# A four-convolution graph network: one block of nodes moved from the dense matrix to the gathered part

## The reference

```
edge_index = stack([src, dst])
h = max(layernorm(x), 0); x = x + L0(h)   # two GATv2 layers: softmax over each target's edges, then sums
h = max(layernorm(x), 0); x = x + L1(h)   # one GCN layer, then a layer norm
h = max(layernorm(x), 0); x = x + L2(h)   # gelu((h[src] + edge_attr) @ W1.T) * bases, summed per target; two norms
h = max(layernorm(x), 0); x = x + L3(h)   # three GCN layers with a skip

def _gcn_conv(x, W, b, src, dst, ew, n):  # used three times in L3; L1 is of the same form
    deg  = segment_sum(ew, dst);  dinv = rsqrt(deg)
    norm = dinv[src] * ew * dinv[dst]
    return segment_sum((x @ W)[src] * norm[:, None], dst) + b
```

## Time and profile before

| | us |
|---|---|
| median of 3 runs | 6614.33 (6613.65 to 6617.98) |
| profiled execution | 6613.22 |
| its span | 6611.4 |
| mean granted clock of PE | 0.760 |

### The profile page before, as it was taken

How to read it: one execution, slowest core, us unless ns; L and a number is a source line. 1 busy time by engine, 2 the same in 40 slices (tenths; PEclk the granted TensorE clock), 3 DMA queues, 4 the chain that set the end, 5 groups by cost and what they waited for, 6 DMA issues and landing times. The chain is left out here.

```text
span 6611.4 us, 98533 instructions
## 1 busy us (share of the span) xinstructions
PE 4901.7 (74%) x22849; PEld 3470.2 (52%) x22849; DVE 4012.6 (61%) x12754; ACT 2179.0 (33%) x5456; POOL 4554.9 (69%) x4402
## 2 busy tenths in 40 slices
PE   3677775457766766555996995666666799999998
PEld 2344443246654444433766995555555455555555
DVE  7998996589976676334776446444444644444444
ACT  4344444359943343343773003222222400000000
POOL 1777777688877777777877662777777177376474
PEclk9555556579965555556997997777777799999999
DMA  5988865457744444333555883655555299899897
GB/s 203 296 297 288 280 183 149 124 105 143 143 71 108 107 106 95 80 81 63 87 84 159 288 286 114 174 160 160 160 160 151 77 303 305 287 305 301 290 305 254
DMA packets 922048, 1211.81 MB, mean 183 GB/s; under 512 B 256572, under 2 KB 658496, under 8 KB 908602
## 3 DMA queue, kind: packets, MB, share of 16 engines
q1 hardware_dynamic: 601694, 867.12, 41.0%
q0 software_dynamic: 205952, 221.31, 17.1%
q10 hardware_dynamic: 113836, 117.04, 5.2%
HBM read 970.24 MB, written 235.93 MB: 182 GB/s over the span
## 5 line engine op out<-in xcount | busy, mean ns | idle before, releaser
L1182 POOL DMA_INDIRECT ACC<-table,TABS x1760 | 1664.8, 946 | 610.1 <-issue 610.1
L1497 POOL DMA_INDIRECT BUF<-table,TABS x888 | 841.7, 948 | 560.8 <-issue 257.0
L1263 POOL DMA_INDIRECT adjacency<-TABS x584 | 934.8, 1601 | 242.2 <-issue 214.4
L1803 POOL DMA_INDIRECT TABS<-table,SPOT_SRC x836 | 788.8, 944 | 317.9 <-issue 317.6
L1988 PE MATMUL picked<-BUF,G 128*128 x2368 | 582.1, 426 | 440.9 <-DVE ACC L2014 386.5
L1988 PEld LDWEIGHTS picked<-BUF,G 128*128 128x128 f32 x2368 | 513.7, 320 | 675.0 <-issue 675.0
L2491 PE MATMUL asum<-BUF 128*128 128x144 f32 x3520 | 558.4, 303 | 122.4 <-DVE BUF L2463 100.2
L1826 PE MATMUL pre<-wmat,BUF 128*128 128x128 f32 x1672 | 325.9, 356 | 357.0 <-DVE BUF L1852 346.8
L1996 DVE TENSOR_TENSOR picked<-picked,ACC 128x512 f32<-128x512 f32 (+1 forms) x440 | 247.3, 562 | 545.2 <-DMA ACC<-table,TABS 499.2
L2491 PEld LDWEIGHTS asum<-BUF 128*128 128x128 f32 x3520 | 472.9, 196 | 197.7 <-issue 180.1
L1212 DVE TENSOR_TENSOR ACC<-ACC,asum 128x144 f32 (+1 forms) x1760 | 463.0, 263 | 151.5 <-DVE ACC L1212 65.0
(11 more groups left out here) (466 smaller groups left out, 9968.3 us busy)
## 6 DMA issues: line engine op xcount, KB each, us to landing
TABS<-adjacency SPq DMA_DIRECT2D x264, 512.0 KB
BUF<-in_edge_pair SPq DMA_DIRECT2D x836, 128.0 KB
BUF<-adjacency SPq DMA_DIRECT2D x99, 1024.0 KB
BUF<-adjacency SPq DMA_DIRECT2D x198, 512.0 KB
adjacency<-zeros ACTq DMA_DIRECT2D x44, 1792.0 KB
G<-adjacency SPq DMA_DIRECT2D x132, 512.0 KB
kept<-ACC SPq DMA_DIRECT2D x220, 272.0 KB, 4.4
G<-kept SPq DMA_DIRECT2D x220, 272.0 KB
```

The source lines that it names most:

```text
L1182: po.indirect_dma_start(rows[:, slot, j, 0:width], None, tab, bass.IndirectOffsetOnAxis(ap=SRC[:, q * GT + j:q * GT + j + 1], axis=0)).the ...
L1263: po.indirect_dma_start(adj_flat, bass.IndirectOffsetOnAxis(ap=PLACE[:, k:k + 1], axis=0), TOTAL[:, k:k + 1], None, compute_op=ALU.add).th ...
L1497: po.indirect_dma_start(R[:, q % deep_ring, j, :], None, table, bass.IndirectOffsetOnAxis(ap=SRC[:, k:k + 1], axis=0)).then_inc(S(f"gather ...
L1803: po.indirect_dma_start(R[:, g % RD, j, :], None, table, bass.IndirectOffsetOnAxis(ap=SPOT_SRC[:, k:k + 1], axis=0)).then_inc(S(f"gathered ...
```

## The change

LIGHT goes from 16 to 17, so 17 blocks are gathered and 32 are dense. From this follow: NEAR 74 to 78 groups, FAR 146 to 142, HEAVY 33 to 32, chunks (DENSE) 9 to 8; the chunk of one block is gone, and the part of one block is now the last light part (the fifth), while the last part is four blocks wide. The adding groups are spread anew by FIRST_FAR and MERGES: 1, 10, 60, 9 in the first GAT layer (before 1, 11, 60, 10), 1, 2, 50 in the second (before 1, 3, 49), and 9 in front of the mixed stage (before 11). In the mixed stage near groups come every 1.1 units (before 1.3), the last at unit 90 of 104 (before 100 of 108); in the last stage every 2.2 units (before 2.5), the last at unit 181 of 200 (before 194 of 207), which is in the last chunk, and the assertion that it lies ahead of the last chunk is replaced.

```diff
--- before.py
+++ after.py
@@ -57,13 +57,13 @@
 CD = 8
 
 CYCLE = NB - 1
-LIGHT = 16
+LIGHT = 17
 HEAVY = NB - LIGHT
 assert SORT_T + NB - 1 <= TILES
 NEAR_TILES = LIGHT * (SORT_T + CYCLE - 1) // CYCLE
 NEAR = -(-NEAR_TILES // (2 * GT)) * 2
 FAR = GROUPS - NEAR
-FIRST_FAR = 82
+FIRST_FAR = 80
 SEGMENTS = ((0, FIRST_FAR), (FIRST_FAR, FAR))
 DENSE = -(-HEAVY // CB)
 PARTS = ([(b, min(CB, LIGHT - b)) for b in range(0, LIGHT, CB)]
@@ -73,7 +73,7 @@
 FIRST = (6, 6, 0)
 BY_VECTOR = 24
 ONES_FROM = 160
-MERGES = ((1, 11, 60, 10), (1, 3, 49, 11))
+MERGES = ((1, 10, 60, 9), (1, 2, 50, 9))
 assert FAR % 2 == 0
 
 
@@ -1288,7 +1288,7 @@
                 w = min(CB, HEAVY - c * CB)
                 deep = CB * CB // w
                 units += [(c, w, b, min(deep, NB - b)) for b in range(0, NB, deep)]
-            places = near_by(6, 1.3)
+            places = near_by(6, 1.1)
             assert places[-1] < len(units)
             added, after_add, after_dense = [0], {}, {}
             finished, total = [], st[0][:, 0:NB]
@@ -1453,8 +1453,8 @@
                 units += [(c, w, b, min(deep, NB - b)) for b in range(0, NB, deep)]
             US = len(units)
             ends = {c: max(n for n, u in enumerate(units) if u[0] == c) for c in range(DENSE)}
-            places = near_by(12, 2.5)
-            assert places[-1] < ends[DENSE - 2]
+            places = near_by(12, 2.2)
+            assert places[-1] + 1.3 * KS < US
             loops_at = {6 + 2 * i: i for i in range(FREE_PARTS)}
             advance_at, n = {}, places[-1] + 3
             for k in range(KS - 1):
```

## The result

The changed kernel takes 6653.15 us (median of 5, 6644.88 to 6660.11) against 6614.33 before: 1.0061 times as long, 95% interval 1.005 to 1.0071. It is slower by about 39 us, where +11 was forecast; the range ended at 6639. The profiled execution, 6660.11 us, is the slowest of the five, 7 us above the median.

The account below looks back on a forecast made before the run. POOL's gathers were to replace PE as the last stage's bound. Last stage +25.7, mixed stage -4.1, stage ends -7.4 and -3.0 sum to +11.2 on the profiled 6613.2, stated as 6625 us; range 6600 to 6639.

Parts of the forecast that it names:

- the bound: Last stage's three passes: POOL's gathers, no longer PE, set each pass's last near product, together +22.7 us.
- The final +3.0: Behind the third pass: the last part is four blocks and not one, +3.0 us (+1.5 to +5).
- the tail at 0: Last near product to each pass's end: length unchanged, 0, between -1.2 a pass and +3.
- the chain of shifts: Last-stage tails: twelve parts of DVE steps, loads and ACT shifts, about 3.3 us a part, put at 43.6 us.
- rival C: Last-stage tails: the chain of shifts, at 3.6 us a part, adds +4 a pass, +12, giving 6637 us; 23%.
- the transition: Last stage, last advance to the next pass's first gather: no term in the forecast, 0.
- the 7.2 us saved: Last stage: PE's work falls 7.2 us a pass, which becomes waiting as it lies ahead of the last near product.
- 20-odd us of thin products: Last stage before the change: part of the 43.9 us from last near product to the pass's end.
- The stage ends: Stage ends with adding groups: fewer POOL steps, -7.4 us in the second dense stage, -3 behind the first maximum.
- The mixed stage: Mixed stage: POOL sets the last near product, chunk 6's add comes first, finish costs +3.0; -4.1 us in all.
- A: Whole kernel: PE stays the bound, with POOL's step under 4.65 us a group; 6563 us; 8%.
- B: Whole kernel: passes cost only +14, mixed stage and stage ends gain in full, -8 and -15; 6605 us; 17%.

Follow-up runs that it names:

- the kernel with fewer gathers: The changed kernel gathering three tiles and not four per group in the last stage, from the first pass's seventh group on (fourth tile stale): 6568.49 us.
- runs without rows: Last-stage dinv row loads left out except the first two (stale rows used): 6622.43 us on the changed kernel, 6592.92 on the kernel before.
- four rows: A ring of four dinv rows and not two, each row asked for two parts earlier: 6629.57 us on the changed kernel, 6592.72 on the kernel before.
- stores first: The changed kernel with the next pass's first two dinv rows loaded behind the last part's store, not ahead of the last three stores: 6642.86 us.
- the four-block store before the change: The kernel before, its last part's store in the first two passes writing four blocks and waiting for the stores ahead of it: 6611.63 us.
- the kernel with 2.4: The kernel before (16 blocks) with near groups every 2.4 units in the last stage and every 1.15 in the mixed stage: 6623.06 us.
- the best one: The kernel before with a ring of four dinv rows and only five parts finished ahead of the mixed stage's add: 6582.14 us.

## Why the prediction was wrong

**Right: the bound.** POOL sets the last near product, +23.5 against +22.7; its step stayed 1.25 us, PE waits 18 us a pass for gathers, and the kernel with fewer gathers is 85 us faster. The final +3.0 was +3.1.

**Wrong: the tail at 0, "between -1.2 a pass (PE alone) and +3".** It grew by 10.6 over the three passes. PE alone was worked out rightly: 42.7 and three units are the 47.9 of the runs without rows and with four. The term that failed is the chain of shifts, taken over from before less two steps: the twelfth shift was to end 41.5 - 1.4 = 40.1 after the near product, and it ended 44.4, 42.5 and 48.0 after it. Its pace is no property of the chain: it waits for rows that land beside the unit loads. With four rows the same shift ends 36.2, 36.3 and 39.4 after the near product. That was rival C, whose sign, place and mechanism were right; its 12 us were 10.6. That they came so close is in part luck: C had +4 in each pass, and the passes have +2.5, -0.8 and +8.9. The third pass loads no units of a next one, and there the unit loads beside the chain went from 5 to 11 and the rows' mean landing from 3.9 to 5.0 us; in the second, 16 loads and not 13 made the rows no later on average. I gave C 23% and let it stand alone.

The wait for rows explains why the forecast of the tail missed, but not why the change is slower, since the kernel before has this wait too (21 us of its tails, against 18 after). With four rows in both, the change still costs 37 us, 6629.57 against 6592.72: 25.7 to the last near product, 13.6 in the tails, 9.3 in the transitions.

**Wrong: no cost for the transition.** The forecast has no term for the way from the last advance to the next first gather. It became 13.5 us longer over two passes. Of 6.8 a pass, 4.4 go when the stores stand ahead of the next pass's rows, and 2.3 when the last store is of one block; both were asked in runs of their own, and that they add up was not tried. The rows were ahead of the stores before too, but earlier: before, the second row's load went out 6.3 us ahead of the last store (5718.07 and 5724.36) and had landed when that store was issued, at 5722.2; after, it went out 4.6 us ahead (5722.76 and 5727.35) and landed at 5729.8, behind the store's issue (landings by the semaphore's updates in the trace; the second pass's end shows the same order). From the last store's issue to POOL's first gather it takes 5.3 and 5.6 us before, 6.5 and 6.2 there with four blocks stored, 7.0 and 6.8 after the change with the stores first, 9.1 and 8.7 with one block behind the rows, and 11.3 and 11.1 with four blocks behind them. So 5.7 of the 6.8 are the landing of the last stores, and 1.1 the wider last advance with its move; 4.4 and 2.3 are more than 5.7, so the two causes overlap.

**The step that failed beneath both** is the sentence that the 7.2 us saved "lie ahead of the last near product", followed by a sum in which everything behind it stays as it is. The thin products are not ahead of it: they are units 200 to 206, and the last near group stood at unit 194. (The prediction's "20-odd us of thin products" are 11 us; the 20 are all products of the tail before.) By the prices of rows 3, as an estimate, what goes from ahead of it is 26 wide products less the new groups and the loop block, 18.5 us a pass, and PE waits 18.1 for gathers. Behind it PE's own work grows from 32.0 us (11 wide products, 49 thin ones, twelve advances, the near group) to 42.7. Before, PE spent most of that difference waiting for shifts; after, it works, and the wait for rows still comes on top.

With PE as the bound, POOL's lead covers a late first gather, as the four-block store before the change shows (transition longer, time the same). With POOL as the bound each pass is a closed ring: first gather, last gather, tail, stores, first gather. Every link counts in full.

**The rest, about right.** The stage ends were put at -10.4. The second logits' first gather came at 1937.3 on average over the seven profiles with 17 blocks (1933.0 to 1944.6) and at 1946.3 over the seven with 16 (1942.9 to 1952.8): -9.0, though the two profiles compared first show only -2.1. The mixed stage was put at -4.1 and is -1.1 from its first gather to L2's (530.7 against 531.9 on average; the kernel with 2.4 and the best one, where that stage differs, left out): the near products ended as forecast, but the last chunk took 45.6 us and not 43.8, and the wait before it 2.2. Together -9.0 - 1.1 + 50.7 = +40.6, and the medians differ by 38.8.

The faster rivals A and B fell with the 395 us of the gathers.

## What to carry to other kernels

When a change hands the bound from one engine to another, work out the new engine's whole loop, with the transfers that close it, and not only the stretch in which it takes over: what the old bound had hidden is paid from then on. A chain's pace read from a trace holds for the transfers that ran beside it; where the change puts more of them there, bound it anew. Count what stands behind the last step that the new bound sets: what is moved there is paid too. And before moving work between two engines, look at what small loads wait for: asking for four rows ahead and not two was worth 19 us in the kernel before, with no work moved.

## What the runs showed of the hardware

The sums stage of the first layer does the same work in all these kernels, and it is through sooner where the granted clock of PE is higher (the clock of a stretch is a mean: its records show 1.0 or 0.5, which is 2.4 or 1.2 GHz). The same stretch before, after, and in the run without rows (the last three columns are the clock, the DMA share and GB/s):

```profile
1395.00:1840.00 445.00, 347.88 (x2108) 298.74 (x2108) 407.84 (x1684) 405.98 (x1273) 373.55 (x230) 0.95 0.71 142
```

```profile
1395.00:1840.00 445.00, 354.43 (x2077) 304.75 (x2075) 402.11 (x1658) 399.06 (x1251) 372.88 (x231) 0.92 0.70 140
```

```profile
1395.00:1840.00 445.00, 345.79 (x2136) 296.09 (x2135) 412.74 (x1707) 410.50 (x1287) 374.48 (x228) 0.96 0.72 144
```

At 0.92 PE gets through 2077 instructions in the stretch, at 0.96 through 2136. The second logits' start moved over 11.6 us between the seven profiles with 17 blocks, which are alike up to there, more than the stage ends were worth: it was 1944.6 and 1943.6 at the two lowest clocks, 0.92 and 0.93, and 1933.0 to 1936.3 at 0.95 to 0.99. Such a gain can't be read from one pair of traces. At the same clock of 0.97 the start is 1934.2 (stores first) and 1943.0 (before, 2.4), 8.8 apart.
